# Two-stage cross-attention on one core: the scores' products by x's high part merged into one 512-column product, with the halves added before the softmax

## The chip, the cores and the metric

The kernel runs on one core of one Trainium2 chip. The metric is the device time in microseconds (us) of one execution, as the median of several runs. A profiled execution has a time of its own and, inside it, a span from its first to its last instruction. Engines are named as in the profile: PE is TensorE's matrix product, PEld its weight load, DVE is VectorE, ACT ScalarE, POOL GpSimd, SP SyncE, whose queue (SPq) issues nearly all DMAs.

## The reference, cut to what matters

There are 16 samples; x and the context are each 256 x 512 per sample. Stage one is a cross-attention without heads, stage two a non-local block whose output is added to stage one's.

```python
q = einsum('blh,oh->blo', x, w_q);  k = einsum('bsh,oh->bso', ctx, w_k);  v = einsum('bsh,oh->bso', ctx, w_v)
scores = einsum('blh,bsh->bls', q, k) / sqrt(512)
context = einsum('bls,bsh->blh', softmax(scores), v)
x1 = x + alpha * einsum('blh,oh->blo', context, w_o)          # stage one
theta, phi, g = conv1x1(x1), conv1x1(ctx), conv1x1(ctx)        # 256 -> 128 channels
y = (theta^T phi / 512) g^T
out = batchnorm(conv1x1(y)) + x1                               # stage two
```

The kernel folds weights first: qk = w_k by w_q and ov = w_v by w_o. The scores are then x times tT, where tT = qk applied to the context. The second stage goes by u (from phi and the context's Gram matrix) and t1 (from u and the folded weights wg).

## The kernel before, in words

Every fp32 factor is held as a high and a low part of type fp32r. ACT writes the high part (`hi`), DVE the low one (`lo`: the source less the high part). A product is then three matmuls per 128-deep tile of the contraction: high by high, high by low, low by high.

The 16 samples are worked in 8 pairs: `pair(0, first=True)`, a loop over pairs 1 to 6, and `pair(7, last=True)`; b is the sample in the pair. Each engine has its own instruction list, run in order and tied to the others by semaphores. In one pair PE runs in this order: `scores(0)`, `scores(1)`, `values(0)` (the product by ov, in PSUM banks 2 and 3), `w_g_phi(0)` and `(1)` (t1, from u), `values(1)`, `delta(0)`, `delta(1)` (attention output), `both_rows` (the Gram matrix of the next pair's context), the `t_tile`s (the next pair's tT), theta, output, and `phi_gram` for the next pair. In the first pair `phi_gram` comes behind the scores and `w_g_phi` behind `delta(1)`.

`scores(b)` (L379 to L391) works two row tiles lt of 128 rows. For each it runs k = 0 to 3, with three 256-column matmuls each (L388 to L390): 24 matmuls for a sample, 48 for a pair. The scores of sample b fill one bank, `SCORE_BANK = [0, 1]`.

Behind them comes the softmax. DVE's `row_maxima(b)` reads the bank (L864) and makes the negated, scaled maximum (L867). ACT's `exp(b)` (L641) reads the bank and writes `probs`, with row sums. DVE's `turn_squares(b)` (L873) turns 32 x 32 squares of `probs` into `blocks`. SP sends `blocks` to DRAM and fetches them back into `pT_raw`, which completes the transpose. `pT_part(b)` splits that, and `delta(b)` needs it.

In pairs 1 to 7 the other chain of importance here is that of u. Behind `row_maxima(1)`, DVE runs `u_rows` (L905, four instructions), then `turn_squares(1)`, the reciprocals `invert_sums` (L879) and `u_part` (L910, which makes `u_lo`). ACT makes `u_hi` behind `exp(1)`. PE waits for `u_lo` ahead of `w_g_phi(0)` (L482).

```python
                row_maxima(0)
                turn_squares(0)
                row_maxima(1)
                if not first:
                    u_rows()
                turn_squares(1)
                for b in range(2):
                    invert_sums(b)
```

Of the kernel before, what the change touches and what calls it, by code (L numbers as in the profile page):

```python
# [8 lines left out]
ACT = mybir.ActivationFunctionType  # L9
# [23 lines left out]
def two_stage_cross_attention(nc, x, x_t, ctx_n, ctx_t, w_q, w_k, w_v, w_o_t, g_w, phi_w_t, theta_w_t,  # L33
                              w_w_t, cols, rows, out):
    with ExitStack() as stack:
# [17 lines left out]
        cT = c_sides[:, :, :, 0], c_sides[:, :, :, 1]  # L53
        tT = split("tT", [P, KH, 2, S])
        vo = split("vo", [P, 2, KS, H])
# [58 lines left out]
        wk = [as_k(t[:]) for t in tT]  # L114
        wq = [by_k(t[:]) for t in vo]
        wv = [by_k(t[:]) for t in x1]
        wo = [as_k(t[:]) for t in xT]

        bank = [stack.enter_context(nc.psum_tensor(f"bank{n}", [P, 512], F32)) for n in range(8)]

        SCORE_BANK = [0, 1]
        VO_BANK = [[2, 3], [6, 7]]
# [6 lines left out]
        GRAM_BANK = [[0, 1], [6, 7]]  # L129
        WG_BANK, WG_BIAS_BANK = 4, 5  # L130
        FIRST_T1_BANK = [6, 7]
# [37 lines left out]
        u_made, u_hi, u_lo = sem("u_made"), sem("u_hi_made"), sem("u_lo_made")  # L169
        scores_done = sem("scores_done")  # L170
        max_made, neg_max_made = sem("max_made"), sem("neg_max_made")
        probs_made, inv_sum_made = sem("probs_made"), sem("inv_sum_made")
# [21 lines left out]
        def _(sp):  # L194
# [61 lines left out]
            def pair(p, first=False, prefetch=True, last=False):  # L256
# [10 lines left out]

                if not first:
                    fetch_phi()
                    next_x(0)  # L270
                for b in range(2):
                    sp.wait_ge(blocks_made, two[b + 1])
                    send(moved[b], blocks[:, b], blocks_stored[b])
                    if not first:
                        sp.wait_ge(blocks_stored[b], turned[16])
                        fetch(pT_raw[:, b], moved[b], pT_loaded[b])
                if first:
                    for b in range(2):
                        sp.wait_ge(blocks_stored[b], turned[16])
                        fetch(pT_raw[:, b], moved[b], pT_loaded[b])  # L280
                    sp.wait_ge(phi_blocks_made, two[2])
                    send(phi_moved, phi_blocks[:], phi_stored)
                    fetch_phi()
                else:
                    next_x(1)
# [46 lines left out]
        def _(pe):  # L332
# [9 lines left out]
            def cut(parts, *at):  # L342
                return tuple(t[at] for t in parts)
# [35 lines left out]
            def scores(b, all_tT=None):  # L379

                for lt in range(KL):
                    dst = bank[SCORE_BANK[b]][:, lt * S:(lt + 1) * S]
                    for k in range(KH):
                        if lt == 0 and k == KH - 1 and all_tT is not None:
                            pe.wait_ge(tT_lo, all_tT)
                        x_hi, x_lo = cut(xT, every, b, k, tile(lt))
                        t_hi, t_lo = cut(tT, every, k, b, every)
                        pe.matmul(dst, x_hi, t_hi, start=(k == 0), stop=False)  # L388
                        pe.matmul(dst, x_hi, t_lo, start=False, stop=False)  # L389
                        mm = pe.matmul(dst, x_lo, t_hi, start=False, stop=(k == KH - 1))  # L390
                mm.then_inc(scores_done, 1)  # L391
# [68 lines left out]
            def pair(p, first=False, last=False):  # L460
                two, four = counts(pe, p, 2, [1, 2, 3, 4]), counts(pe, p, 4, [-2, 0, 2, 3, 4, 5, 6])
                pe.wait_ge(tT_lo, four[3])
                pe.wait_ge(xT_lo, two[1])
                scores(0, four[4])
                pe.wait_ge(xT_lo, two[2])
                if not first:
                    pe.wait_ge(out_made, four[-2])
                scores(1)
                if first:
                    pe.wait_ge(small_lo, 2)  # L470
                    for b in range(2):
                        pe.wait_ge(gram_lo, b + 1)
                        phi_gram(b, FIRST_PHI_BANK)
                else:
                    pe.wait_ge(v_made, two[2])
                for st in range(KS):
                    values(0, st)
                if first:
                    pe.wait_ge(v_made, two[2])
                else:  # L480
                    pe.wait_ge(out_made, four[0])
                    pe.wait_ge(u_lo, p + 1)  # L482
                    w_g_phi(0)
                    w_g_phi(1)
# [4 lines left out]
                for lt in range(KL):  # L489
                    delta(0, lt)  # L490
                if first:
                    pe.wait_ge(wg_lo, 1)
                    pe.wait_ge(wg_bias_made, 1)
                else:
                    pe.wait_ge(t1_made, two[2])
# [61 lines left out]
        def _(act):  # L557
# [68 lines left out]
            def gram_part(b, count, pairs_read=None):  # L626
# [3 lines left out]
                hi(gram[0][:, b], gram_raw[:, b], gram_hi)  # L630

            act.wait_ge(c_summed, 4)
            for b in range(2):
                gram_part(b, KS * (b + 1))

            def pair(p, first=False, last=False):
                loads = counts(act, p, 16, [32])
                landed = counts(act, p, 16 * BLOCKS, [16 * BLOCKS])
                two, four = counts(act, p, 2, [-1, 0, 1, 2, 3]), counts(act, p, 4, range(-2, 9))

                def exp(b):  # L641
                    act.wait_ge(neg_max_made, two[b + 1])
                    if not first:
                        act.wait_ge(pT_lo, two[-1 + b])
                    for lt in range(KL):
                        e = act.activation(probs[:, b, lt], bank[SCORE_BANK[b]][:, lt * S:(lt + 1) * S], ACT.Exp,  # L646
                                           bias=neg_max[:, b, lt:lt + 1], scale=SCALE,
                                           accum_out=row_sum[:, b, lt:lt + 1])
                    e.then_inc(probs_made, 1)
# [36 lines left out]

                exp(0)
                exp(1)
                if first:
                    act.wait_ge(wg_done, 1)  # L690
                    hi(wg[0][:], bank[WG_BANK][:].rearrange("p (k l) -> p k l", k=KS), wg_hi)
                    hi(wg_bias[:], bank[WG_BIAS_BANK][:, 0:L], wg_bias_made)
                else:
                    u_part()
# [3 lines left out]
                if not first:  # L698
# [3 lines left out]
                    t1_part(1)  # L702
                pT_part(1)
                vo_part(1, 0)
                vo_part(1, 1)
                if first:
# [48 lines left out]
        def _(dve):  # L755
# [101 lines left out]
            def pair(p, first=False, last=False):  # L857
# [92 lines left out]

                row_maxima(0)
                turn_squares(0)
                row_maxima(1)
                if not first:
# [4 lines left out]
                if first:  # L959
                    lo(wg, wg_hi, 1, (every,), bank[WG_BANK][:].rearrange("p (k l) -> p k l", k=KS), wg_lo)  # L960
                    phi_squares(0, 1, FIRST_PHI_BANK)
                    phi_squares(1, 2, FIRST_PHI_BANK)
                else:
                    u_part()
# [3 lines left out]
                if not first:  # L968
# [3 lines left out]
                    t1_part(1)  # L972
                pT_part(1)
                vo_part(1, 0)
                vo_part(1, 1)
                if first:
# [109 lines left out]
```

## Time and profile before

| | us |
|---|---|
| time, median of 3 runs | 393.51 (393.35 to 393.60) |
| the profiled execution's own time | 393.05 |
| its span | 391.3 |
| busy: PE, PEld, DVE, ACT, POOL | 385.3, 329.9, 292.7, 188.3, 1.3 |
| the chain that ended last | PE 96%, DVE 2%, DMA 1% |

Busy time of PE is the time in which at least one matmul is recorded; consecutive matmuls overlap in the records, so the step between two starts tells the rate, not the duration of one. Pairs follow each other every 44.63 to 44.64 us by the starts of their scores (133.52, 178.16, 222.79 and so on).

### The profile page before, as it was taken

What the parts mean: (1) busy time and instruction counts of PE and PEld (TensorE: products, weight loads), DVE (VectorE), ACT (ScalarE), POOL (GpSimd) and SP (SyncE); (2) the same over time, 40 slices, a digit from 0 to 9 for tenths busy, and PEclk for the clock granted to TensorE, in tenths of its full rate; (3) what the DMA queues carried; (4) which work ended last, traced back from release to release, by engine and by line L of the source; (5) the groups of instructions that cost most, each with busy time, mean ns of one, the idle gap of its engine ahead of it and who ended that gap; (6) DMA issues with size and microseconds to landing.
All of it is one profiled execution on the core that took longest, in us unless ns stands there. A gap on an engine that the chain in (4) does not pass through costs nothing.

```text
span 391.3 us, 5851 instructions
## 1 busy us (share of the span) xinstructions
PE 385.3 (98%) x1981; PEld 329.9 (84%) x1981; DVE 292.7 (75%) x573; ACT 188.3 (48%) x390; POOL 1.3 (0%) x6
## 2 busy tenths in 40 slices
PE   8999999999999999999999999999999999999995
PEld 5888988889888988889888898889888898889884
DVE  5898657986598766886688756895678955896675
ACT  4477543662655256641646237451656237451342
POOL 1000000000000000000000000000000000000000
PEclk9999999999999999999999999999999999999999
DMA  7985740577473655546463566455474453024423
GB/s 236 371 316 196 261 134 29 169 260 229 125 264 91 238 158 188 176 146 234 125 230 107 204 182 204 153 169 203 126 245 123 175 190 118 27 80 164 133 80 107
DMA packets 56363, 68.13 MB, mean 174 GB/s; under 512 B 4640, under 2 KB 47136, under 8 KB 53280
## 3 DMA queue, kind: packets, MB, share of 16 engines
q1 hardware_dynamic: 56064, 67.59, 52.4%
q10 hardware_dynamic: 288, 0.39, 0.3%
q8 instruction: 6, 0.10, 0.1%
q14 instruction: 5, 0.04, 0.0%
HBM read 49.09 MB, written 18.87 MB: 174 GB/s over the span
## 4 chain that ended last, share of the span: by engine, by line
PE 96%; DVE 2%; DMA 1%; ACT 0%; issue 0%; DVEq 0%; ACTq 0%
PE bank L337 24%; PE bank L338 24%; PE bank L339 24%; PE bank L400 7%; PE bank L368 6%; PE bank L389 4%; PE bank L388 4%; PE bank L390 4%; DMA cT_raw<-w_q 1%; DVE xb L921 0%; DVE xb L947 0%; DVE x_lo L759 0%; ACT x_hi L559 0%; DVE xb L1012 0%; DVE vo_hi L766 0%
## 5 line engine op out<-in xcount | busy, mean ns | idle before, releaser
L337 PE MATMUL bank<-ov_hi,c_sides 128*128 128x512 f32 x128 | 50.0, 390 | 0.0
L338 PE MATMUL bank<-ov_lo,c_sides 128*128 128x512 f32 x128 | 50.0, 390 | 0.0
L338 PE MATMUL bank<-c_sides,qk_hi 128*128 128x512 f32 x128 | 50.0, 390 | 0.0
L339 PE MATMUL bank<-c_sides,qk_lo 128*128 128x512 f32 x128 | 49.9, 390 | 0.0
L337 PE MATMUL bank<-c_sides,qk_hi 128*128 128x512 f32 x128 | 49.8, 389 | 0.0
L339 PE MATMUL bank<-ov_hi,c_sides 128*128 128x512 f32 x128 | 49.8, 389 | 0.0
L646 ACT ACTIVATE probs<-bank,neg_max 128x256 f32<-128x256 f32 x32 | 14.9, 471 | 57.0 <-DVE neg_max L867 57.0
L759 DVE TENSOR_TENSOR vo_lo<-bank,vo_hi 128x512 fp32r<-128x512 f32 x32 | 21.9, 689 | 20.3 <-ACT vo_hi L559 20.3
L559 ACT ACTIVATE x_hi<-xb 128x512 fp32r<-128x512 f32 x32 | 20.0, 633 | 34.6 <-DVE xb L921 34.5
L389 PE MATMUL bank<-tT_lo,xT_hi 128*128 128x256 f32 x128 | 36.2, 283 | 0.0
L390 PE MATMUL bank<-tT_hi,xT_lo 128*128 128x256 f32 x128 | 36.2, 283 | 0.0
L388 PE MATMUL bank<-tT_hi,xT_hi 128*128 128x256 f32 x128 | 36.2, 283 | 0.0
L559 ACT ACTIVATE tT_hi<-bank 128x512 fp32r<-128x512 f32 x32 | 19.0, 594 | 23.6 <-PE bank L339 23.3
L559 ACT ACTIVATE vo_hi<-bank 128x512 fp32r<-128x512 f32 x32 | 18.8, 594 | 23.9 <-PE bank L339 23.4
L339 PEld LDWEIGHTS bank<-ov_hi,c_sides 128*128 128x128 f32 x128 | 24.0, 188 | 5.1
L339 PEld LDWEIGHTS bank<-c_sides,qk_lo 128*128 128x128 f32 x128 | 24.0, 188 | 5.1
L337 PEld LDWEIGHTS bank<-c_sides,qk_hi 128*128 128x128 f32 x128 | 24.0, 188 | 4.8
L338 PEld LDWEIGHTS bank<-c_sides,qk_hi 128*128 128x128 f32 x128 | 24.0, 188 | 4.8
L337 PEld LDWEIGHTS bank<-ov_hi,c_sides 128*128 128x128 f32 x128 | 24.1, 188 | 4.6
L759 DVE TENSOR_TENSOR tT_lo<-bank,tT_hi 128x512 fp32r<-128x512 f32 x32 | 22.0, 688 | 7.8 <-ACT tT_hi L559 7.8
L338 PEld LDWEIGHTS bank<-ov_lo,c_sides 128*128 128x128 f32 x128 | 24.1, 188 | 4.4
L400 PE MATMUL bank<-c_sides 128*128 128x512 f32 (+1 forms) x128 | 27.6, 366 | 0.0
(137 smaller groups left out, 871.3 us busy)
## 6 DMA issues: line engine op xcount, KB each, us to landing
cT_raw<-ctx_t SPq DMA_DIRECT2D x8, 1024.0 KB, 4.9
xT_raw<-x_t SPq DMA_DIRECT2D x8, 1024.0 KB, 4.8
c_raw<-ctx_n SPq DMA_DIRECT2D x8, 1024.0 KB, 6.8
xb<-x SPq DMA_DIRECT2D x16, 512.0 KB, 4.3
out<-xb SPq DMA_DIRECT2D x14, 512.0 KB, 2.7
gram_moved<-gram_blocks SPq DMA_DIRECT2D x16, 256.0 KB, 2.4
gram_blocks<-gram_moved SPq DMA_DIRECT2D x64, 64.0 KB, 2.0
moved<-blocks SPq DMA_DIRECT2D x16, 256.0 KB, 2.5
```

Of the source, the lines that this page charges most:

```text
L337: pe.matmul(dst, ahi, bhi, start=(k == 0), stop=False)
L338: pe.matmul(dst, ahi, blo, start=False, stop=False)
L339: mm = pe.matmul(dst, alo, bhi, start=False, stop=(k == k_tiles - 1))
L368: mm = pe.matmul(bank[KH * n + m][:], lhs[a][:, k, tile(m)], rhs[b][:, k, :], start=(k == 0 and a == b), stop=(k == KH - 1 and a == 1))
L388: pe.matmul(dst, x_hi, t_hi, start=(k == 0), stop=False)
L389: pe.matmul(dst, x_hi, t_lo, start=False, stop=False)
L390: mm = pe.matmul(dst, x_lo, t_hi, start=False, stop=(k == KH - 1))
L400: mm = pe.matmul(bank[GRAM_BANK[b][i]][:, i * P:], cT[0][:, k, b, tile(i)], c_sides[:, k, b].rearrange("p h s -> p (h s)")[:, i * P:], sta ...
L559: act.activation(dst, src, ACT.Identity, **more).then_inc(made, 1)
L646: e = act.activation(probs[:, b, lt], bank[SCORE_BANK[b]][:, lt * S:(lt + 1) * S], ACT.Exp, bias=neg_max[:, b, lt:lt + 1], scale=SCALE, ac ...
L759: dve.tensor_tensor(parts[1][at], src, parts[0][at].bitcast(F32), ALU.subtract).then_inc(made, 1)
```

## The change

In words, in the order of the diff:

- `tT`'s two parts become the two sides of one tensor `t_sides`, so that the high and the low 256 columns of one k lie next to each other.
- All eight PSUM banks become one tensor, and the scores of a sample take two banks: 0 and 1 for sample 0, 4 and 5 for sample 1. Each row tile has a bank, its left half for what tT's high part meets and its right half for x's high by tT's low.
- `scores`: per k one 512-column matmul of x's high part by both parts of tT, and one 256-column matmul of x's low part by tT's high part into the left half; 16 matmuls per sample instead of 24.
- The softmax gets two steps ahead of it. ACT's `low_scores(b)` copies the right halves into `probs`; DVE adds the left halves to them in `probs`; maximum and exp then read `probs` (SBUF) instead of PSUM. The steps of ACT are ordered `low_scores(0)`, `exp(0)`, `low_scores(1)`, `exp(1)`.
- Banks and waits follow: the wait for the last pair's `out_made` is taken up to `scores(0)` in part, and `w_g_phi`, which uses banks 4 and 5, waits for sample 1's sums. The weight product `w_g_bias` uses banks 3 and 2, so in the first pair the waits for wg stand ahead of `values(0)`.
- First pair: SP sends phi's blocks between the two sends of the softmax, and both fetches follow behind them; wg's low part and the phi squares are taken up in DVE's list; a small exp is run in ACT's set-up.
- Pairs 1 to 7: `vo_part(1, 0)` runs ahead of `pT_part(1)`.

```diff
-        tT = split("tT", [P, KH, 2, S])
+        t_sides = sb("t_sides", [P, KH, 2, 2, S], F32R)
+        tT = t_sides[:, :, :, 0], t_sides[:, :, :, 1]
...
-        SCORE_BANK = [0, 1]
+        banks = stack.enter_context(nc.psum_tensor("bank", [P, 8, 512], F32))
+        bank = [banks[:, n] for n in range(8)]
+
+        SCORE_BANK = [slice(0, 2), slice(4, 6)]
...
-        WG_BANK, WG_BIAS_BANK = 4, 5
+        WG_BANK, WG_BIAS_BANK = 3, 2
...
-                if not first:
+                def send_squares(b):
+                    sp.wait_ge(blocks_made, two[b + 1])
+                    send(moved[b], blocks[:, b], blocks_stored[b])
+
+                def fetch_squares(b):
+                    sp.wait_ge(blocks_stored[b], turned[16])
+                    fetch(pT_raw[:, b], moved[b], pT_loaded[b])
+
+                if first:
+                    send_squares(0)
+                    sp.wait_ge(phi_blocks_made, two[2])
+                    send(phi_moved, phi_blocks[:], phi_stored)
+                    send_squares(1)
+                    fetch_squares(0)
+                    fetch_squares(1)
+                    fetch_phi()
+                else:
...
-                    dst = bank[SCORE_BANK[b]][:, lt * S:(lt + 1) * S]
+                    dst = banks[:, SCORE_BANK[b]][:, lt]
...
-                        t_hi, t_lo = cut(tT, every, k, b, every)
-                        pe.matmul(dst, x_hi, t_hi, start=(k == 0), stop=False)
-                        pe.matmul(dst, x_hi, t_lo, start=False, stop=False)
-                        mm = pe.matmul(dst, x_lo, t_hi, start=False, stop=(k == KH - 1))
+                        if k > 0:
+                            pe.matmul(dst[:, 0:S], x_lo, tT[0][:, k, b], start=False, stop=False)
+                        mm = pe.matmul(dst, x_hi, t_sides[:, k, b].rearrange("p h s -> p (h s)"),
+                                       start=(k == 0), stop=(k == KH - 1))
+                        if k == 0:
+                            pe.matmul(dst[:, 0:S], x_lo, tT[0][:, k, b], start=False, stop=False)
...
                 pe.wait_ge(tT_lo, four[3])
                 pe.wait_ge(xT_lo, two[1])
+                if not first:
+                    pe.wait_ge(out_made, four[-2])
                 scores(0, four[4])
                 pe.wait_ge(xT_lo, two[2])
                 if not first:
-                    pe.wait_ge(out_made, four[-2])
+                    pe.wait_ge(out_made, four[0])
                 scores(1)
...
+                    pe.wait_ge(wg_lo, 1)
+                    pe.wait_ge(wg_bias_made, 1)
...
-                    pe.wait_ge(out_made, four[0])
+                    pe.wait_ge(scores_summed, two[2])
                     pe.wait_ge(u_lo, p + 1)
...
+            act.activation(neg_max[:, 0], std_col[:], ACT.Exp)
...
+                def low_scores(b):
+                    act.wait_ge(scores_done, two[b + 1])
+                    if not first:
+                        act.wait_ge(pT_lo, two[-1 + b])
+                    hi(probs[:, b], banks[:, SCORE_BANK[b], S:2 * S], low_scores_copied)
...
-                        e = act.activation(probs[:, b, lt], bank[SCORE_BANK[b]][:, lt * S:(lt + 1) * S], ACT.Exp,
+                        e = act.activation(probs[:, b, lt], probs[:, b, lt], ACT.Exp,
...
-                exp(0)
-                exp(1)
+                low_scores(0)
                 if first:
                     act.wait_ge(wg_done, 1)
...
-                else:
+                exp(0)
+                low_scores(1)
+                exp(1)
+                if not first:
                     u_part()
...
                 def row_maxima(b):
-                    dve.wait_ge(scores_done, two[b + 1])
-                    dve.tensor_reduce(row_max[:, b], bank[SCORE_BANK[b]][:].rearrange("p (t s) -> p t s", t=KL),
-                                      AX.X, ALU.max).then_inc(max_made, 1)
+                    dve.wait_ge(low_scores_copied, two[b + 1])
+                    dve.tensor_tensor(probs[:, b], banks[:, SCORE_BANK[b], 0:S], probs[:, b],
+                                      ALU.add).then_inc(scores_summed, 1)
+                    dve.wait_ge(scores_summed, two[b + 1])
+                    dve.tensor_reduce(row_max[:, b], probs[:, b], AX.X, ALU.max).then_inc(max_made, 1)
...
                 row_maxima(0)
+                if first:
+                    lo(wg, wg_hi, 1, (every,), bank[WG_BANK][:].rearrange("p (k l) -> p k l", k=KS), wg_lo)
                 turn_squares(0)
                 row_maxima(1)
-                if not first:
+                if first:
+                    phi_squares(0, 1, FIRST_PHI_BANK)
+                    phi_squares(1, 2, FIRST_PHI_BANK)
+                else:
                     u_rows()
                 turn_squares(1)
                 for b in range(2):
                     invert_sums(b)
...
-                pT_part(1)
+                if first:
+                    pT_part(1)
                 vo_part(1, 0)
+                if not first:
+                    pT_part(1)
                 vo_part(1, 1)
```

## Rows read from the trace of the kernel before

**Rows 1.** The page's first two parts: busy us (share) xinstructions; granted clock, 40 slices.
```profile
PE 385.3 (98%) x1981; PEld 329.9 (84%) x1981; DVE 292.7 (75%) x573; ACT 188.3 (48%) x390; POOL 1.3 (0%) x6
...
PEclk9999999999999999999999999999999999999999
```

**Rows 2.** PE's waits over the whole span: engine line, waited for, us, times, longest.
```profile
PE bank L337 <- DVE x_lo L759: 0.9, 1, 0.9
PE bank L352 <- PEq L1080: 0.8, 1, 0.8
PE bank L368 <- DVE vo_hi L766: 0.2, 1, 0.2
```

**Rows 3.** Timeline of PE, pair 2: first product of scores, values(0), w_g_phi; start, us, engine.
```profile
133.52 0.28 PE L388 MATMUL bank<-tT_hi,xT_hi 128*128 128x256 f32 x1
...
139.27 0.40 PE L337 MATMUL bank<-ov_hi,c_sides 128*128 128x512 f32 x1
...
144.74 0.28 PE L337 MATMUL bank<-wg_hi,u_hi 128*128 128x256 f32 x1
```

**Rows 4.** Timeline of DVE in pair 2, from out_rows to u_lo and the second vo_lo.
```profile
133.06 1.42 DVE L947 SCALAR_TENSOR_TENSOR xb<-bank,out_bias,xb 128x512 f32<-128x512 f32 x2
136.59 0.69 DVE L864 TENSOR_REDUCE row_max<-bank 128x2 f32<-128x512 f32 x1 [2.11 <-PE bank L390]
137.32 0.17 DVE L867 TENSOR_SCALAR neg_max<-row_max 128x2 f32<-128x2 f32 x1
138.75 0.71 DVE L873 STREAM_TRANSPOSE blocks<-probs 128x512 f32<-128x512 f32 x1 [1.26 <-ACT probs L646]
139.47 0.69 DVE L864 TENSOR_REDUCE row_max<-bank 128x2 f32<-128x512 f32 x1
...
140.30 1.14 DVE L905 SCALAR_TENSOR_TENSOR phi_blocks<-row,gram_raw,phi_blocks 128x128 f32<-128x128 f32 x4
141.45 0.71 DVE L873 STREAM_TRANSPOSE blocks<-probs 128x512 f32<-128x512 f32 x1
142.09 0.18 DVE L879 RECIPROCAL inv_sum<-row_sum 128x2 f32<-128x2 f32 x2
142.19 0.67 DVE L910 TENSOR_TENSOR u_lo<-phi_blocks,u_hi 128x512 fp32r<-128x512 f32 x1
...
145.57 0.69 DVE L759 TENSOR_TENSOR vo_lo<-bank,vo_hi 128x512 fp32r<-128x512 f32 x1 [2.02 <-ACT vo_hi L559]
```

**Rows 5.** Timeline of ACT in pair 2: exp(0), exp(1), u_hi (from SBUF), second vo_hi (from PSUM).
```profile
137.60 0.48 ACT L646 ACTIVATE probs<-bank,neg_max 128x256 f32<-128x256 f32 x1 [6.09 <-DVE neg_max L867]
...
140.40 0.47 ACT L646 ACTIVATE probs<-bank,neg_max 128x256 f32<-128x256 f32 x1 [1.78 <-DVE neg_max L867]
...
141.48 0.63 ACT L559 ACTIVATE u_hi<-phi_blocks 128x512 fp32r<-128x512 f32 x1
...
144.94 0.60 ACT L559 ACTIVATE vo_hi<-bank 128x512 fp32r<-128x512 f32 x1 [2.12 <-PE bank L339]
```

**Rows 6.** The page's groups: 512 columns from PSUM by DVE and by ACT.
```profile
L759 DVE TENSOR_TENSOR vo_lo<-bank,vo_hi 128x512 fp32r<-128x512 f32 x32 | 21.9, 689 | 20.3 <-ACT vo_hi L559 20.3
...
L559 ACT ACTIVATE vo_hi<-bank 128x512 fp32r<-128x512 f32 x32 | 18.8, 594 | 23.9 <-PE bank L339 23.4
```

**Rows 7.** Timeline of DVE and PE at the one late wait of PE: its restart.
```profile
381.29 1.29 DVE L759 TENSOR_TENSOR x_lo<-xb,x_hi 128x512 fp32r<-128x512 f32 x2
...
382.64 0.38 PE L337 MATMUL bank<-x_hi,theta_w_hi 128*128 128x256 f32 x1 [0.88 <-DVE x_lo L759]
382.86 0.28 PE L338 MATMUL bank<-x_lo,theta_w_hi 128*128 128x256 f32 x1
```

**Rows 8.** Timeline of DVE and PE in the last pair: last vo_lo and the start of delta(1).
```profile
375.70 1.28 DVE L759 TENSOR_TENSOR vo_lo<-bank,vo_hi 128x512 fp32r<-128x512 f32 x2
...
377.52 0.39 PE L337 MATMUL bank<-vo_hi,pT_hi 128*128 128x512 f32 x1
```

**Rows 9.** Timeline of ACT in the first pair: the load of exp's table, and exp(0).
```profile
46.35 1.28 ACT L646 ACT_TABLE_LOAD   x1
47.91 0.47 ACT L646 ACTIVATE probs<-bank,neg_max 128x256 f32<-128x256 f32 x1 [0.27 <-DVE neg_max L867]
```

More of the change, by code:

```diff
@@ L113, in two_stage_cross_attention @@
         wv_raw, wo_raw = as_k(xT_raw[:]), by_k(c_raw[:])
-        wk = [as_k(t[:]) for t in tT]
+        t_flat = t_sides[:].rearrange("p k b h s -> p (k b h s)")
+        wk = [t_flat[:, n * KH * H:(n + 1) * KH * H].rearrange("p (k n) -> p k n", k=KH) for n in range(2)]
         wq = [by_k(t[:]) for t in vo]
@@ L117, in two_stage_cross_attention @@
         wo = [as_k(t[:]) for t in xT]
-        bank = [stack.enter_context(nc.psum_tensor(f"bank{n}", [P, 512], F32)) for n in range(8)]
-        SCORE_BANK = [0, 1]
+        banks = stack.enter_context(nc.psum_tensor("bank", [P, 8, 512], F32))
+        bank = [banks[:, n] for n in range(8)]
+        SCORE_BANK = [slice(0, 2), slice(4, 6)]
         VO_BANK = [[2, 3], [6, 7]]
@@ L170, in two_stage_cross_attention @@
         scores_done = sem("scores_done")
+        low_scores_copied, scores_summed = sem("low_scores_copied"), sem("scores_summed")
         max_made, neg_max_made = sem("max_made"), sem("neg_max_made")
@@ L266, in next_x @@
                     load_x(p, b)
-                if not first:
+                def send_squares(b):
[13 more added lines that the diff above has]
+                else:
                     fetch_phi()
                     next_x(0)
-                for b in range(2):
-                    sp.wait_ge(blocks_made, two[b + 1])
-                    send(moved[b], blocks[:, b], blocks_stored[b])
-                    if not first:
[L275 to L283, printed above, removed]
-                else:
+                    send_squares(0)
+                    fetch_squares(0)
+                    send_squares(1)
+                    fetch_squares(1)
                     next_x(1)
@@ L490, in pair @@
                     delta(0, lt)
[L491 to L494, printed above, removed]
+                if not first:
                     pe.wait_ge(t1_made, two[2])
@@ L639, in pair @@
                 two, four = counts(act, p, 2, [-1, 0, 1, 2, 3]), counts(act, p, 4, range(-2, 9))
+                def low_scores(b):
[3 more added lines that the diff above has]
+                    hi(probs[:, b], banks[:, SCORE_BANK[b], S:2 * S], low_scores_copied)
                 def exp(b):
                     act.wait_ge(neg_max_made, two[b + 1])
-                    if not first:
-                        act.wait_ge(pT_lo, two[-1 + b])
                     for lt in range(KL):
-                        e = act.activation(probs[:, b, lt], bank[SCORE_BANK[b]][:, lt * S:(lt + 1) * S], ACT.Exp,
+                        e = act.activation(probs[:, b, lt], probs[:, b, lt], ACT.Exp,
                                            bias=neg_max[:, b, lt:lt + 1], scale=SCALE,
@@ L692, in pair @@
                     hi(wg_bias[:], bank[WG_BIAS_BANK][:, 0:L], wg_bias_made)
-                else:
+                exp(0)
+                low_scores(1)
+                exp(1)
+                if not first:
                     u_part()
@@ L702, in pair @@
                     t1_part(1)
-                pT_part(1)
+                if first:
+                    pT_part(1)
                 vo_part(1, 0)
+                if not first:
+                    pT_part(1)
                 vo_part(1, 1)
@@ L951, in pair @@
                 row_maxima(0)
+                if first:
+                    lo(wg, wg_hi, 1, (every,), bank[WG_BANK][:].rearrange("p (k l) -> p k l", k=KS), wg_lo)
                 turn_squares(0)
                 row_maxima(1)
-                if not first:
+                if first:
+                    phi_squares(0, 1, FIRST_PHI_BANK)
+                    phi_squares(1, 2, FIRST_PHI_BANK)
+                else:
                     u_rows()
@@ L958, in pair @@
                     invert_sums(b)
[L959 to L963, printed above, removed]
+                if not first:
                     u_part()
@@ L972, in pair @@
                     t1_part(1)
-                pT_part(1)
+                if first:
+                    pT_part(1)
                 vo_part(1, 0)
+                if not first:
+                    pT_part(1)
                 vo_part(1, 1)
```

## The prediction

> **What bounds the kernel now.** I read the page's first parts, then who waited for whom on PE, then the timeline of one pair from the middle of the run. The first shows PE busy 98% of the span, the granted clock full in every slice [rows 1]. The second shows that PE waits three times in the whole run, twice in the first microseconds and once in the last pair [rows 2]. So in the pairs PE never starves: every other engine's work is covered, and the span is the sum of PE's steps. A change can gain only by making PE's list shorter, and loses as soon as one of PE's operands comes later than PE does. The third view gives both quantities, the rate of the products and how early each operand lies ready.
>
> **What the products give.** The scores of pair 2 run from 133.52 to 139.27, 5.75 us for 48 products of 256 columns: 0.1198 each. `values(0)` runs from 139.27 to 144.74, 5.47 us for 24 products of 512 columns: 0.2279 each [rows 3]. The columns don't change (3 x 256 become 512 + 256), but a product has a fixed part beside its columns, and one of three goes. A k step costs 3 x 0.1198 = 0.3594 now and 0.2279 + 0.1198 = 0.3477 then; 16 steps in a pair save 0.187 us, 8 pairs 1.5 us. That is all the change can earn: 393.5 - 1.5 = 392.0. The new order of the two products in a k step and the new layout of tT change no column count, so they cost nothing.
>
> The Trainium skill speaks against even this gain. "TensorE: Matmul & The Clock Gate", section "Back-to-back issue gap", gives the gap of a warm product as its columns at 2.4 GHz plus 2.5 ns. By that, a product fewer saves 2.5 ns, 0.04 us a pair and 0.3 us in all. The rows have 0.1198 and 0.2279, that is 13 and 15 ns above their columns at 2.4 GHz, so the trace disagrees with the page and I keep 0.187.
>
> **What it puts on the softmax's chain.** Before `w_g_phi`, PE waits for `u_lo`. Now `u_lo` ends at 142.19 + 0.67 = 142.86, and PE arrives at 144.74 [rows 3, 4]: 1.88 us of slack. DVE makes it in order behind both `row_maxima` and both `turn_squares`, so all that is added to those delays it. Worked out step by step for pair 2, from an unchanged start at 133.52:
>
> - `scores(0)` is done after 8 steps of 0.3477, at 136.30. ACT starts 0.20 behind PE's last step (144.74 to 144.94) [rows 3, 5], at 136.50, and copies 512 columns from PSUM in 0.594 [rows 6], to 137.09.
> - DVE follows an ACT result after 0.03 (144.94 + 0.60 to 145.57) [rows 4, 5], at 137.12; the add costs 0.689 as `vo_lo` does, also one operand from PSUM and one from SBUF [rows 6]: 137.81. With the 0.04 that DVE takes to see its own semaphore (136.59 + 0.69 to 137.32), the maximum starts at 137.85. It started at 136.59 [rows 4]: 1.26 late.
> - From there to `turn_squares(0)` it took 138.75 - 136.59 = 2.16: 140.01. The maximum and the exps now read SBUF. For ACT the nearest rows are 0.63 from SBUF against 0.60 from PSUM [rows 5], for DVE 0.67 against 0.689 [rows 4, 6]; two exps and one maximum give +0.02 to +0.04. I take 140.03.
> - ACT copies sample 1's half behind `exp(0)`, about 139.9 to 140.5, just under cover of `turn_squares(0)`. The add follows that by the 0.64 from turn to reciprocal (141.45 to 142.09) [rows 4], at 140.67, and the second maximum by 0.73, at 141.40 instead of 139.47: 1.93 late.
> - `u_rows`, `exp(1)`, `turn_squares(1)`, the reciprocals and `u_lo` follow as before [rows 4]: `u_lo` starts at 142.19 + 1.93 + 0.02 = 144.14 and ends at 144.81.
> - PE restarts 0.06 behind the operand that it waits for (381.29 + 1.29 = 382.58 to 382.64), and its first 256-column product then takes 0.22 to the next instead of 0.12 [rows 7]: 0.16 together, so as if it began at 144.97.
>
> PE arrives 0.19 earlier than it did, at 144.55, and so waits 0.42 us. The pair ends 144.97 - 144.74 = 0.23 us later than before. As long as that wait is there, what PE saves in the scores is worth nothing: the chain sets the time, and PE stands. This holds for the 7 pairs that run `w_g_phi` here: +1.6 us.
>
> Bounds of the 0.23: `exp(1)` starts 0.93 after its maximum, `exp(0)` 1.01 (139.47 to 140.40, 136.59 to 137.60) [rows 4, 5], and if the copy ahead of `exp(0)` takes up that difference 0.08 go. The maxima from SBUF may save 0.02 more each, and the 0.10 of the first product may be hidden: together -0.22, or +0.01 a pair. On the other side, the second add may follow the turn by 0.72 as the maximum did (138.75 to 139.47), 0.08 more, and the exps may cost 0.04 each from SBUF: +0.16, or +0.39 a pair.
>
> The Trainium skill's table in "VectorE: DVE Perf Modes", section "The TRN2 errata — SBUF-src ops pay a fixed extra latency per instruction", has VectorE's fixed part 62 cycles (0.065 us) smaller from SBUF than from PSUM and ScalarE's 52 cycles (0.043 us) larger. By it, two maxima and about three exps on the chain come to nothing, 0.02 us off my sum for a pair; the rows show the same signs, at 0.02 and 0.03.
>
> **The other edits.** The new waits for `out_made` ahead of the scores cost nothing: its last instruction ends at 134.48 [rows 4], and `scores(1)`, which now needs it, begins at 133.52 + 2.78 = 136.30. The wait for sample 1's sums stands with that for `u_lo` and is met 3 us sooner. `values(1)` and everything behind stand behind the wait for `u_lo` and shift with it. The added ACT and DVE work (2 x 0.594 and 2 x 0.689 a pair) and the later sends shift `pT` by 1.3 to 2 us, and SP's fetches of sample 0, the send and the fetches of sample 1, the next x and the next context's load behind them. The narrowest place I see is `delta(1)` in the last pair: the last `vo_lo` ends at 376.98 and PE begins at 377.52 [rows 8], 0.54 us. PE comes 0.23 later there too and one ACT step is taken up ahead of `pT_part(1)`, so I cost it at nothing. If its cover is gone it costs what the chain exceeds that by, at most about 0.5 a pair.
>
> In the first pair `w_g_phi` comes late, so no such wait arises, and the 0.19 is gained. The table load of 1.28 moves out of the way of `exp(0)` [rows 9], which makes up for the added copy and add; but `fetch(0)` now stands behind `send(1)` on SP, and `values(0)` behind `wg_lo`, which by the same steps is ready just as PE arrives. I bound the pair at -0.19 to 0 and take -0.1.
>
> **The sum.** 393.05 for the profiled execution (391.3 span and 1.75 around it), + 7 x 0.23 - 0.1 = +1.5: 394.6. The median lay 0.46 above that execution, so 395.0. With +0.01 and +0.39 a pair the same case reaches from 393.4 to 396.3.
>
> **The rivals.**
>
> - *The wait does not arise (faster).* If `u_lo` ends by 144.39, PE finds it ready at 144.55 and keeps all its saving: 392.0. The point from which it decides is a delay of the chain of 1.53 us, where I have 1.95. For it: 0.42 is a small remainder of twelve estimated steps. Against: no single step has that much to give, and all my lower bounds together leave 0.20.
> - *The merged product does not do what it says.* If a 512-column product beside a 256-column one costs what three small ones cost, `scores(0)` is done at 136.39, the chain ends 0.09 later, and the pair is +0.32: 393.5 + 2.2 = 395.7. For it: the Trainium skill's 2.5 ns, told above. Against: the two rates in the rows.
> - *A second wait.* The later `pT` and `vo` parts, not only `u`, miss PE in every pair: 0.3 to 0.5 us more each, 397 to 398.5. For it: 0.54 us of cover in the last pair. Against: PE comes later too.
>
> **Chances.** My forecast 0.68 (0.20 of it within 0.2% of before, 0.48 slower), the wait that does not arise 0.15, no gain from the merging 0.10, a second wait 0.07. About 0.2%, 0.8 us, is what a measurement of this kernel can tell from no change. Faster 0.15, same 0.20, slower 0.65. The range from 391.9 to 396.6 takes in the first three cases and leaves out the second wait and the margins of the rest.
>
> **What would show it.** In the profile after: first products of scores and values 5.56 us apart; among PE's waits a new row, `w_g_phi` for DVE's `u_lo`, seven times, 0.2 to 0.6 each; `u_lo` ending 11.2 to 11.4 us after the pair's first score; pairs 44.7 to 45.0 us apart (44.63 before). If that row is missing and the pairs are 44.45 apart, my chain is too long. If the scores still take 5.75, the product's price is wrong. A wait of `delta` for `pT_lo` or `vo_lo` would be the third rival.

## The result and the profile after

The changed kernel takes 395.51 us (median of 6 runs, 395.14 to 396.00), beside 393.43 for the kernel before in as many runs; the ratio is 1.0056 with a 95% interval of 1.0043 to 1.0069. It is slower by 2.1 us. The prediction was 395.0, slower, with a range from 391.9 to 396.6.

The page's first two parts of the changed kernel (the columns are those of [rows 1]):

```profile
PE 385.7 (98%) x1853; PEld 322.0 (82%) x1853; DVE 302.2 (77%) x589; ACT 197.2 (50%) x407; POOL 1.3 (0%) x6
...
PEclk9999999999999999999999999999999999999999
```

128 products are gone, and PE's busy time is not shorter but 0.4 us longer. Of PE's waits, the view of [rows 2]:

```profile
PE bank L347 <- DVE u_lo L935: 1.2, 6, 0.2
PE bank L347 <- DVE x_lo L782: 0.9, 1, 0.9
...
PE bank L347 <- issue: 0.2, 1, 0.2
PE bank L412 <- DVE c_sides L782: 0.2, 1, 0.2
```

The top row is new: `w_g_phi` waits for `u_lo` (six times in this view; the steps below show a shorter seventh pause in the last pair). Its 1.2 us look like too little, and they are. A 512-column product is recorded with 0.39 us, though the next one starts 0.23 later, so the first 0.16 us of every pause lie under the record of the product before it. The size of a pause must be read from the steps between starts. PE's timeline in pair 2, to be laid beside [rows 3]:

```profile
133.78 0.39 PE L399 MATMUL bank<-t_sides,xT_hi 128*128 128x512 f32 x1
...
139.41 0.39 PE L347 MATMUL bank<-ov_hi,c_sides 128*128 128x512 f32 x1
...
145.22 0.38 PE L347 MATMUL bank<-wg_hi,u_hi 128*128 128x256 f32 x1 [0.21 <-DVE u_lo L935]
145.44 0.28 PE L348 MATMUL bank<-wg_lo,u_hi 128*128 128x256 f32 x1
...
178.74 0.39 PE L399 MATMUL bank<-t_sides,xT_hi 128*128 128x512 f32 x1
```

The scores now take 5.63 us (133.78 to 139.41) instead of 5.75. `values(0)` takes 5.81 instead of 5.47, and `w_g_phi`'s first product has 0.22 to the next instead of 0.12. The pair is 44.96 us long instead of 44.64. The timelines of ACT (the copy) and of DVE in the same pair, beside [rows 4, 5], show why:

```profile
136.87 0.60 ACT L572 ACTIVATE probs<-bank 128x512 f32<-128x512 f32 x1 [5.12 <-PE bank L399]
```
```profile
137.50 0.69 DVE L887 TENSOR_TENSOR probs<-bank,probs 128x512 f32<-128x512 f32 x1 [2.78 <-ACT probs L572]
138.23 0.69 DVE L890 TENSOR_REDUCE row_max<-probs 128x2 f32<-128x512 f32 x1
...
140.38 0.71 DVE L898 STREAM_TRANSPOSE blocks<-probs 128x512 f32<-128x512 f32 x1 [1.26 <-ACT probs L664]
141.01 0.66 DVE L887 TENSOR_TENSOR probs<-bank,probs 128x512 f32<-128x512 f32 x1
141.70 0.69 DVE L890 TENSOR_REDUCE row_max<-probs 128x2 f32<-128x512 f32 x1
...
143.75 0.71 DVE L898 STREAM_TRANSPOSE blocks<-probs 128x512 f32<-128x512 f32 x1
...
144.49 0.67 DVE L935 TENSOR_TENSOR u_lo<-phi_blocks,u_hi 128x512 fp32r<-128x512 f32 x1
```

Counted from the pair's first score, `u_lo` ends at 144.49 + 0.67 - 133.78 = 11.38, where it ended at 9.34. PE goes on at 11.44, 0.06 behind it.

### The profile page after: what moved, and what is told of

It reads as the page before. It is cut to its first block, busy times and chain, and to the rows that moved or that the text cites. A ratio compares the mean times of both kernels' runs of the same rounds, so it can differ in the third digit from the quotient of the medians.

```text
span 393.4 us, 5634 instructions
## 1 busy us (share of the span) xinstructions
PE 385.7 (98%) x1853; PEld 322.0 (82%) x1853; DVE 302.2 (77%) x589; ACT 197.2 (50%) x407; POOL 1.3 (0%) x6
## 4 chain that ended last, share of the span: by engine, by line
PE 83%; DVE 8%; issue 4%; ACT 3%; DMA 1%; DVEq 0%; ACTq 0%
PE bank L347 22%; PE bank L348 21%; PE bank L349 21%; PE bank L412 7%; PE bank L378 6%; PE bank L399 5%; ACT probs L664 2%; DVE row_max L890 2%; DVE probs L887 2%; PE bank L398 2%; ACT probs L572 1%; DVE u_lo L935 1%; DMA cT_raw<-w_q 1%; PE bank L402 1%; DVE neg_max L892 1%
## 5 line engine op out<-in xcount | busy, mean ns | idle before, releaser
L399 PE MATMUL bank<-t_sides,xT_hi 128*128 128x512 f32 x128 | 44.0, 396 | 0.0
L572 ACT ACTIVATE t_sides<-bank 128x512 fp32r<-128x512 f32 x32 | 19.0, 593 | 23.5 <-PE bank L349 23.4
L664 ACT ACTIVATE probs<-probs,neg_max 128x256 f32<-128x256 f32 x32 | 16.0, 502 | 27.8 <-DVE neg_max L892 27.8
L782 DVE TENSOR_TENSOR t_sides<-bank,t_sides 128x512 fp32r<-128x512 f32 x32 | 22.0, 686 | 7.7 <-ACT t_sides L572 7.6
L412 PE MATMUL bank<-c_sides 128*128 128x512 f32 (+1 forms) x128 | 27.6, 366 | 0.2 <-DVE c_sides L782 0.2
L572 ACT ACTIVATE probs<-bank 128x512 f32<-128x512 f32 x16 | 9.4, 586 | 35.8 <-PE bank L399 35.8
L398 PE MATMUL bank<-t_sides,xT_lo 128*128 128x256 f32 x96 | 27.1, 282 | 0.0
L412 PEld LDWEIGHTS bank<-c_sides 128*128 128x128 f32 x128 | 23.5, 188 | 3.6 <-DVE c_sides L782 0.4
```

Source lines behind the costliest of these rows:

```text
L398: pe.matmul(dst[:, 0:S], x_lo, tT[0][:, k, b], start=False, stop=False)
L399: mm = pe.matmul(dst, x_hi, t_sides[:, k, b].rearrange("p h s -> p (h s)"), start=(k == 0), stop=(k == KH - 1))
L412: mm = pe.matmul(bank[GRAM_BANK[b][i]][:, i * P:], cT[0][:, k, b, tile(i)], c_sides[:, k, b].rearrange("p h s -> p (h s)")[:, i * P:], sta ...
L572: act.activation(dst, src, ACT.Identity, **more).then_inc(made, 1)
L664: e = act.activation(probs[:, b, lt], probs[:, b, lt], ACT.Exp, bias=neg_max[:, b, lt:lt + 1], scale=SCALE, accum_out=row_sum[:, b, lt:lt ...
L782: dve.tensor_tensor(parts[1][at], src, parts[0][at].bitcast(F32), ALU.subtract).then_inc(made, 1)
```

## Experiments

The theory: copy and add stand on the chain to `u_lo`, which now ends later than PE comes, and PE stands until then in each pair. The rivals: the merged products or the two banks cost the time themselves; the added load of ACT and DVE slows the pair as such; or the softmax's data come too late as well. Pairs are compared by the starts of the scores of pairs 2 and 3.

**Without copy and add.** DVE's `row_maxima` and ACT's `exp` read the left half of the scores' banks, and `low_scores` is gone from ACT's list. DVE's part of the edit:

```diff
-                    dve.wait_ge(low_scores_copied, two[b + 1])
-                    dve.tensor_tensor(probs[:, b], banks[:, SCORE_BANK[b], 0:S], probs[:, b],
-                                      ALU.add).then_inc(scores_summed, 1)
-                    dve.wait_ge(scores_summed, two[b + 1])
-                    dve.tensor_reduce(row_max[:, b], probs[:, b], AX.X, ALU.max).then_inc(max_made, 1)
+                    dve.wait_ge(scores_done, two[b + 1])
+                    dve.tensor_reduce(row_max[:, b], banks[:, SCORE_BANK[b], 0:S], AX.X, ALU.max).then_inc(max_made, 1)
```

> The changed kernel with its merged products, but without the copy by ACT and the add by DVE: maximum and exp read the left half of the scores' banks straight from PSUM. It leaves out of the scores the product of x's high part by tT's low part (PE still makes it). Theory of the late operand (PE waits 0.43 us a pair for u_lo because copy, add and their handoffs delay it by 2 us): u_lo is ready before PE comes, no wait, pairs 44.63 - 0.115 = 44.52 us apart, 8 x 0.115 = 0.9 us under the kernel before, about 392.5. Rival, that the merged products or the two banks themselves cost the time: pairs stay at about 44.9 and the time above 394.5.

Measured: 391.45 us, ratio 0.9946 (0.9933 to 0.9959). The first of PE's waits, of which the others are under 0.9 us and not for `u_lo`, and then its timeline in pairs 2 and 3:

```profile
PE bank L347 <- DVE x_lo L776: 0.9, 1, 0.9
```
```profile
133.01 0.39 PE L399 MATMUL bank<-t_sides,xT_hi 128*128 128x512 f32 x1
...
144.08 0.28 PE L347 MATMUL bank<-wg_hi,u_hi 128*128 128x256 f32 x1
...
177.51 0.39 PE L399 MATMUL bank<-t_sides,xT_hi 128*128 128x512 f32 x1
```

The wait for `u_lo` is gone and the pairs are 44.50 apart. The merged product thus earns 0.14 us a pair, slightly more than the 0.115 by which the scores' phase had shrunk. `w_g_phi` begins 11.07 after the first score, without waiting. The rival that the merged products or the banks cost the time falls. The median is 1 us under the expectation. In the profiled executions the span from the first score to the end is 1.3 us shorter than before instead of 0.9: 0.14 a pair instead of 0.115, and a first pair that is 0.30 shorter (46.18 against 46.48). The other 0.6 us of the 1.9 between the medians doesn't show in the two profiles, and its cause is open.

**Three products again, with copy and add.**

```diff
-                        if k > 0:
-                            pe.matmul(dst[:, 0:S], x_lo, tT[0][:, k, b], start=False, stop=False)
-                        mm = pe.matmul(dst, x_hi, t_sides[:, k, b].rearrange("p h s -> p (h s)"),
-                                       start=(k == 0), stop=(k == KH - 1))
-                        if k == 0:
-                            pe.matmul(dst[:, 0:S], x_lo, tT[0][:, k, b], start=False, stop=False)
+                        pe.matmul(dst[:, 0:S], x_hi, tT[0][:, k, b], start=(k == 0), stop=False)
+                        pe.matmul(dst[:, 0:S], x_lo, tT[0][:, k, b], start=False, stop=False)
+                        mm = pe.matmul(dst[:, S:2 * S], x_hi, tT[1][:, k, b], start=False, stop=(k == KH - 1))
```

> The changed kernel with its copy, its add and its two banks per sample, but with three 256-column products a k step as before (x's high part by tT's high into the left half, x's low by tT's high into the left, x's high by tT's low into the right). Nothing is left out. PE's list is 0.145 us a pair longer than the changed kernel's (0.115 in the scores, 0.03 in values(0)). Theory of the late operand: only that half of the scores' saving which lies ahead of the chain counts, 0.06 us a pair: pairs 45.02 apart, PE's wait for u_lo 0.1 shorter. Rival, that what PE saves counts in full beside the wait: pairs 45.10 apart.

Measured: 395.45 us, ratio 1.0038 (1.0022 to 1.0054). The first scores of pairs 2 and 3:

```profile
134.36 0.28 PE L397 MATMUL bank<-t_sides,xT_hi 128*128 128x256 f32 x1
...
179.37 0.28 PE L397 MATMUL bank<-t_sides,xT_hi 128*128 128x256 f32 x1
```

45.01 us, not 45.10. Merging the products or not changes a pair by 0.05 us as long as the chain through the softmax sets the time, against 0.14 where PE does. By whole-kernel time the two can't be told apart (395.45 and 395.51).

**One copy more on the chain.**

```diff
+                    if b == 0:
+                        hi(probs[:, b], banks[:, SCORE_BANK[b], S:2 * S], extra_copied)
+                        act.wait_ge(extra_copied, copies)
                     hi(probs[:, b], banks[:, SCORE_BANK[b], S:2 * S], low_scores_copied)
```

> The changed kernel with sample 0's low half copied twice by ACT, one after the other with a wait between, about 0.63 us more ahead of the chain to u_lo in every pair, same result. Theory of the late operand: all of it shows in each of the 7 pairs that wait, 7 x 0.63 = +4.4 us, about 399.9, pairs 45.59 apart. Rival, that ACT at 50% busy has room for it: within 0.3 us of 395.5.

Measured: 400.17 us, ratio 1.0172 (1.0154 to 1.0189). PE's first wait and its timeline, pairs 2 and 3:

```profile
PE bank L348 <- DVE u_lo L941: 5.8, 7, 0.9
```
```profile
134.73 0.39 PE L400 MATMUL bank<-t_sides,xT_hi 128*128 128x512 f32 x1
...
146.79 0.39 PE L348 MATMUL bank<-wg_hi,u_hi 128*128 128x256 f32 x1 [0.83 <-DVE u_lo L941]
...
180.31 0.39 PE L400 MATMUL bank<-t_sides,xT_hi 128*128 128x512 f32 x1
```

The pairs are 45.58 apart, 0.62 more than in the changed kernel: what is put ahead of `exp(0)` shows in full, although ACT is busy half the time. This is the slope of the chain, and it is 1.

**The operand taken up.** First ACT's list, then DVE's:

```diff
                 low_scores(1)
-                exp(1)
                 if not first:
                     u_part()
+                exp(1)
...
                 turn_squares(0)
+                if not first:
+                    u_rows()
                 row_maxima(1)
...
                 else:
-                    u_rows()
+                    u_part()
                 turn_squares(1)
                 for b in range(2):
                     invert_sums(b)
-                if not first:
-                    u_part()
```

> The changed kernel with u's chain taken up: in pairs 1 to 7 DVE runs u_rows between turn_squares(0) and row_maxima(1), ACT makes u_hi ahead of exp(1), DVE u_lo ahead of turn_squares(1). Nothing is left out. Theory of the late operand: u_lo ends about 10.7 us after the pair's first score instead of 11.37, PE comes at 11.10, no wait; pairs 44.52 apart if the softmax of sample 1, now 1.2 us later, still meets delta(1) in time: about 392.7. Rival of a second wait: delta(1) then waits 0.3 to 0.6 us for pT_lo or vo_lo in each pair and the time stays at 395 or above.

Measured: 392.17 us, ratio 0.9972 (0.9961 to 0.9982): faster than both kernels. DVE in pair 2, and PE in pairs 2 and 3:

```profile
140.52 1.10 DVE L930 SCALAR_TENSOR_TENSOR phi_blocks<-row,gram_raw,phi_blocks 128x128 f32<-128x128 f32 x4
...
143.08 0.69 DVE L935 TENSOR_TENSOR u_lo<-phi_blocks,u_hi 128x512 fp32r<-128x512 f32 x1
144.31 0.71 DVE L898 STREAM_TRANSPOSE blocks<-probs 128x512 f32<-128x512 f32 x1 [0.54 <-ACT probs L664]
```
```profile
133.29 0.39 PE L399 MATMUL bank<-t_sides,xT_hi 128*128 128x512 f32 x1
...
144.36 0.28 PE L347 MATMUL bank<-wg_hi,u_hi 128*128 128x256 f32 x1
...
177.78 0.39 PE L399 MATMUL bank<-t_sides,xT_hi 128*128 128x512 f32 x1
```

`u_lo` ends at 10.48 after the first score and PE takes it at 11.07 without a stop. The price is that `turn_squares(1)` comes at 11.02 instead of 9.97. `delta(1)` has room for that: the pairs are 44.49 apart, as without copy and add. So all the added work is still there and costs nothing in pairs 2 to 6, once its place is right. The rival of the load as such falls with this run, and so does that of a second wait in pairs 2 to 6.

**The reader moved instead.**

```diff
-                else:
-                    pe.wait_ge(scores_summed, two[2])
-                    pe.wait_ge(u_lo, p + 1)
-                    w_g_phi(0)
-                    w_g_phi(1)
                 for st in range(KS):
                     values(1, st)
+                if not first:
+                    pe.wait_ge(scores_summed, two[2])
+                    pe.wait_ge(u_lo, p + 1)
+                    w_g_phi(0)
+                    w_g_phi(1)
```

Here DVE's `t1_rows` and the `t1_part`s of both engines follow behind `vo_part(1, 1)`.

> The changed kernel with the reader moved instead of the operand: in pairs 1 to 7 PE runs w_g_phi behind values(1), 5.5 us later, and DVE and ACT make t1's rows and parts behind the vo parts. Softmax and u keep their order and are as late as before. Theory of the late operand: the wait for u_lo is gone though u_lo still ends 11.4 us after the first score; pairs 44.52 apart, about 392.7. Rival, that the added load of ACT and DVE as such slows the pair: still about 44.9 us a pair and 395.

Measured: 394.36 us, ratio 1.0024 (1.0006 to 1.0042), 1.7 us above the expectation; the twelve runs spread from 392.43 to 396.33, and the profiled one took 395.85. PE's first wait; its timeline at the first of them (pair 1) and at the first scores of pairs 2 and 3; and DVE's timeline ahead of that wait:

```profile
PE bank L347 <- DVE blocks L957: 2.3, 2, 1.7
```
```profile
111.25 0.50 PE L347 MATMUL bank<-vo_hi,pT_hi 128*128 128x512 f32 x1 [1.68 <-DVE blocks L957]
...
135.19 0.39 PE L399 MATMUL bank<-t_sides,xT_hi 128*128 128x512 f32 x1
...
179.69 0.39 PE L399 MATMUL bank<-t_sides,xT_hi 128*128 128x512 f32 x1
```
```profile
109.12 0.69 DVE L912 TENSOR_TENSOR pT_lo<-probs,pT_hi 128x512 fp32r<-128x512 f32 x1 [1.31 <-ACT pT_hi L572]
...
110.33 0.86 DVE L957 SCALAR_TENSOR_TENSOR blocks<-wg_bias,v,bank 128x256 f32<-128x256 f32 x2
```

In pairs 2 to 6 the expectation holds to 0.02 us: the wait for `u_lo` is gone though `u_lo` is as late as ever, and the pairs are 44.50 apart. I had not priced what the moved step queues behind. `delta(1)` needs `t1_rows`, these now stand behind `pT_part(1)` on DVE, and in pairs 1 and 7 ACT waits for the softmax's fetched squares (1.37 and 4.01 us). By the steps, `delta(1)` begins 1.84 us late in pair 1 and 0.76 in the last pair, where theta then waits for `x_lo` as well; pair 1 and the last pair are each 2.0 us longer than without copy and add. The fastest of the twelve runs, 392.43, lies at the expected 392.7, so the new waits seem to hang on when the transfers land; with one profile this isn't shown. That `u_lo` is the cause holds; moving the reader is the worse cure.

**The order of the products.** On the kernel with the operand taken up:

```diff
-                    for k in range(KH):
...
+                    for part, k in ((0, 0), (1, 0), (1, 1), (1, 2), (1, 3), (0, 1), (0, 2), (0, 3)):
...
```

> The kernel with u's chain taken up (e3_u_early), the products of a row tile in the order 512, four 256, three 512 instead of 512, 256, 256, 512, 256, 512, 256, 512 columns: two changes of width instead of six. Nothing is left out. The scores now take 5.63 us where 16 steps of 0.3477 make 5.56. Theory that a change of width costs: the phase shrinks to about 5.58 and pairs come 44.45 apart instead of 44.50. Rival, that a product with this operand is slower whatever stands beside it: 5.63 as now.

Measured: 392.43 us, ratio 0.9971 (0.9959 to 0.9983). Pair 2's first score and first product of `values(0)`:

```profile
134.00 0.39 PE L400 MATMUL bank<-t_sides,xT_hi 128*128 128x512 f32 x1
...
139.62 0.39 PE L347 MATMUL bank<-ov_hi,c_sides 128*128 128x512 f32 x1
```

5.62 us against 5.63, pairs 44.50 apart: at most 0.02 of the 0.07 that were to be explained. The changes of width are not what keeps the scores above 5.56. The other expectation, that a product with this operand is slower, is left as the one not refuted; what makes it so is open.

**The first pair's edits undone,** again on the kernel with the operand taken up (SP's order, the phi squares' place, no exp in the set-up; the weights' low part stays where the change put it). DVE's part, which puts the phi squares behind `turn_squares(1)`, is left out here:

```diff
-            act.activation(neg_max[:, 0], std_col[:], ACT.Exp)
...
                     send_squares(0)
-                    sp.wait_ge(phi_blocks_made, two[2])
-                    send(phi_moved, phi_blocks[:], phi_stored)
                     send_squares(1)
                     fetch_squares(0)
                     fetch_squares(1)
+                    sp.wait_ge(phi_blocks_made, two[2])
+                    send(phi_moved, phi_blocks[:], phi_stored)
                     fetch_phi()
```

> e3_u_early with the first pair's edits undone: SP's order (both sends, both fetches, then phi's send and fetch), the phi squares behind turn_squares(1), and no exp in ACT's set-up. Nothing is left out. In e3_u_early the first pair takes 46.52 us, 0.3 of it a wait for the low part of the next context. If these edits earn nothing the pair stays at 46.5 and the time at 392.2. If they were needed, exp(0) comes about 0.9 us later by the table load of 1.28 us and phi's blocks about 1.5 us later, u_lo with them, and the pair takes 47.3 to 48 us: 393.0 to 393.7.

Measured: 394.32 us, ratio 1.0017 (1.0007 to 1.0028), above the expected 393.0 to 393.7 and 2.1 us more than with the edits. By the ratios, each against the kernel before as measured beside it, it is 1.8 us more. PE's first scores of pairs 0 and 1, ACT's table load, and DVE's `u_rows`:

```profile
42.63 0.40 PE L399 MATMUL bank<-t_sides,xT_hi 128*128 128x512 f32 x1
...
90.92 0.39 PE L399 MATMUL bank<-t_sides,xT_hi 128*128 128x512 f32 x1
```
```profile
47.82 1.28 ACT L663 ACT_TABLE_LOAD   x1
```
```profile
64.29 1.14 DVE L929 SCALAR_TENSOR_TENSOR phi_blocks<-row,gram_raw,phi_blocks 128x128 f32<-128x128 f32 x4 [1.62 <-DMA phi_blocks<-phi_moved]
```

The first pair takes 48.29 us against 46.52 with the edits, somewhat above the expected 47.3 to 48. DVE sits 1.62 us waiting for phi's blocks, and behind it PE waits for `u_lo` and for the next context's low part (0.3 and 0.9 in the view of its waits). The table load hardly matters: `exp(0)` starts 6.48 after the pair's first score (49.11) against 6.21 with the edits, 0.27 later where I expected 0.9, because the load (47.82 to 49.10) runs mostly beside DVE's maximum, whose last step ends at 48.80. So these edits are not the loss; beside the longer softmax they save 1.8 us of the first pair, once. How the three share it wasn't tried one by one.

## Why the prediction was right, point by point

**The mechanism and its place** are as forecast: PE waits for `u_lo` ahead of `w_g_phi`, and the saving in the scores buys nothing there. The run without copy and add removes the wait, the one with a copy more lengthens it by the copy, and the run with `u` taken up keeps all the work and loses the wait.

**The chain, step by step,** against the predicted times, both from the first score: first add 3.60 predicted, 3.72 measured; first maximum 4.33 and 4.45; `turn_squares(0)` 6.51 and 6.60; second maximum 7.88 and 7.92; `u_lo` starts 10.62 and 10.71, ends 11.29 and 11.38. Of the 0.12 at the head, 0.03 is the slower scores and 0.08 ACT, which starts its copy 0.28 behind PE's step (136.87, with `scores(0)` half of 5.63) where I had taken 0.20. Over the rest, 0.03 came back. PE's restart cost 0.06 + 0.10 as in [rows 7]. Against a list of PE that runs through (`w_g_phi` at 11.07 and 0.12 to its second product), the pause is 11.44 - 11.07 + 0.10 = 0.47 us; I had 0.42.

**The term that was mis-sized** is the products' saving: 0.187 us a pair predicted, 0.14 measured (44.64 to 44.50 without the wait). I took the rate of a 512-column product from one phase and let it stand beside 256-column ones; the scores take 5.63 where that makes 5.56. So the pair became 0.32 us longer (0.47 - 0.145), not 0.23. Five of the seven waiting pairs show exactly this, 44.95 or 44.96 apart, the last 0.2.

**The cover that I costed at nothing** failed once. I had named the last pair's 0.54 us as the narrowest place; pair 1 had less. There, in the kernel before, the last `vo_lo` ends at 109.40 and `delta(1)` begins at 109.72, 0.32 us of cover:

```profile
108.12 1.28 DVE L759 TENSOR_TENSOR vo_lo<-bank,vo_hi 128x512 fp32r<-128x512 f32 x2
...
109.72 0.39 PE L337 MATMUL bank<-vo_hi,pT_hi 128*128 128x512 f32 x1
```

In pair 1 of the changed kernel `delta(1)` has a wait of its own. DVE's last step before it, and PE's timeline there:

```profile
109.07 0.68 DVE L782 TENSOR_TENSOR vo_lo<-bank,vo_hi 128x512 fp32r<-128x512 f32 x1
```
```profile
109.26 0.39 PE L349 MATMUL bank<-vo_hi,pT_lo 128*128 128x512 f32 x1
109.85 0.47 PE L347 MATMUL bank<-vo_hi,pT_hi 128*128 128x512 f32 x1 [0.20 <-issue]
```

The releaser is named "issue", but `vo_lo` ends at 109.75 and PE goes on at 109.85. That is the third rival, in one pair of seven; pair 1 is 0.52 longer than the pairs behind it, at the 0.5 us that I had bounded such a wait with. The trace shows ACT's `pT_part(0)` late, then the four sums of the context, then `vo_part(1, 0)`; that this order makes the wait is read from the trace and was not tried. The run with three products shows no such wait in pair 1, nor does the one with the operand taken up (0.29 of cover), while the one with another order of products does (pair 1 is 44.79 long, the others 44.50). So it seems to hang on how the transfers fall in the execution.

Pair 1 differs in `u` as well. Before the change `u_lo` ended there at 99.72 and PE took it at 100.10: 0.38 us of slack, not the 1.88 of the other pairs, because DVE's `u_rows` had waited for phi's blocks:

```profile
97.19 1.14 DVE L905 SCALAR_TENSOR_TENSOR phi_blocks<-row,gram_raw,phi_blocks 128x128 f32<-128x128 f32 x4 [1.46 <-DMA phi_blocks<-phi_moved]
```

That wait took up most of the softmax's delay (with the slack it makes 1.46 + 0.38 = 1.84), so PE's pause for `u_lo` came out there much as in the others. I had carried pair 2's slack to pair 1 unread; that the price fitted was luck.

**The sum.** By the profiled executions: 395.14 - 393.05 = 2.09, where I had 1.5. Pair 0 gives +0.09 (I took -0.1: its saving of 0.16 in the scores is lost again in a wait of 0.29 for the next context's low part, `c_sides` L412 among the waits; nor did the moved table load make up for copy and add, as I had it: `exp(0)` starts 6.21 after the first score where it started at 5.50), pair 1 +0.86, pairs 2 to 6 +0.32 each, the last +0.2, together 2.8. The remaining -0.7 lies ahead of the first score (41.72 against 42.41). The six other runs that share the changed kernel's set-up have their first score at 42.16 to 42.53, so it is this execution's and not the change's (next section but one). In the profile, then, the pairs cost 2.8 where my sum had 1.5, just beyond the 2.7 that my +0.39 a pair allows; the wait in pair 1 makes up 0.5 of it, and the start-up hides 0.7. That the total fell so near the forecast is partly luck. The two medians, 2.08 apart, hold such luck on both sides, so I can't say from them whether the true cost is nearer 2.1 or 2.8.

**The rivals.** The wait did arise; the deciding delay that I gave for it was 1.53 us, and the chain came 2.04 later (11.38 against 9.34). The merged product does what it says, at three quarters of its price. The Trainium skill ("TensorE: Matmul & The Clock Gate", section "Back-to-back issue gap") gives its formula for an isolated product; the 0.04 us a pair that I estimated from it for a stream disagrees with the measured 0.14. The Trainium skill's table in "VectorE: DVE Perf Modes", section "The TRN2 errata — SBUF-src ops pay a fixed extra latency per instruction", has VectorE 0.065 us faster from SBUF; the maximum took 0.69 from either. It has ScalarE 0.043 slower, and the exps went from 471 to 502 ns by the page's groups, so there sign and size roughly agree.

## What to carry to other kernels

On an engine that never waits, a saving is worth its price only until the next operand is late: before a change lengthens another engine's chain, list for each operand how long before its reader it is ready, and spend no more than the smallest of these. Read it in every repetition, not in one: pair 1 had the least cover for `delta(1)`, and I had looked at pair 2 and the last. In the other pairs the slack of `u_lo` was 1.88 us and 2 us were put on it; moving `u`'s four small steps ahead of the second maximum gave the slack back and turned +0.56% into -0.28%. When a step is moved, price what it comes to stand behind, too: moving the reader cured the same wait and made a new one in two pairs.

## What was not expected of the hardware

- The start-up differs between executions. PE's first products on real operands, the timeline of the kernel before and then that of the changed one:

```profile
4.59 1.84 PE L368 MATMUL bank<-vo_hi,tT_hi 128*128 128x512 f32 x4 [0.24 <-DVE vo_hi L766]
6.27 1.09 PE L368 MATMUL bank<-vo_lo,tT_hi 128*128 128x512 f32 x4
```
```profile
4.57 1.17 PE L378 MATMUL bank<-vo_hi,t_sides 128*128 128x512 f32 x4 [0.27 <-DVE vo_hi L789]
5.58 1.07 PE L378 MATMUL bank<-vo_lo,t_sides 128*128 128x512 f32 x4
```

  The first four products took 0.42 us each before (512 columns at 1.2 GHz are 0.43) and 0.25 each after, while the granted clock of both pages is full. In both, the constant products ahead of them (0.78 to 3.72) step at 0.43. These four make 0.67 of the 0.69 us between the two first scores. In the nine profiles of this case the first score falls between 41.72 and 42.63, which is 0.9 us where the change costs 2.1, so pairs should be compared, not spans.
- PE's first product after a wait has 0.22 us to the next instead of 0.12, in every pair that waits. In these runs a wait of PE so costs 0.10 more than its length.
- A wait's row under PE shows only what the recorded tail of the last product leaves over: 1.2 us where the steps show 0.47 a pair.
